# Delta-rule layers: tiles of 32 tokens of all four sequences in place of tiles of 128 tokens of one

## The reference

```
h = layer_norm(x, ln_g, ln_b)
qkvb = einsum('sbi,oi->sbo', h, slow_w).reshape(slen, bsz, H, 3 * D + 1)
q, k, v, beta = split(qkvb, [D, 2 * D, 3 * D])
q = softmax(q); k = softmax(k); beta = sigmoid(beta)
def step(W, inp):
    qt, kt, vt, bt = inp
    wk = einsum('bhde,bhe->bhd', W, kt)
    v_new = bt * (vt - wk)
    W = W + einsum('bhd,bhe->bhde', v_new, kt)
    return W, einsum('bhde,bhe->bhd', W, qt)
```

## Time and profile before

| | us |
|---|---|
| runs | 5360.01, 5378.66, 5394.14 |
| median | 5378.66 |
| span of the profiled execution | 5373.4 |
| TensorE busy | 4530.5 (84%), 57100 matmul records |
| VectorE busy | 2972.1 (55%) |
| ScalarE busy | 2152.0 (40%) |
| GpSimd busy | 831.7 (15%) |

### The profile page before, as it was taken

How to read it: one execution, slowest core, us unless ns; L and a number is a source line. 1 busy time by engine, 2 the same in 40 slices (tenths; PEclk the granted TensorE clock), 3 DMA queues, 4 the chain that set the end, 5 groups by cost and what they waited for, 6 DMA issues and landing times. The chain is left out here.

```text
span 5373.4 us, 139944 instructions
## 1 busy us (share of the span) xinstructions
PE 4530.5 (84%) x57100; PEld 2834.8 (53%) x57101; DVE 2972.1 (55%) x5849; ACT 2152.0 (40%) x4091; POOL 831.7 (15%) x2139
## 2 busy tenths in 40 slices
PE   3679898887997888897688886799999999984995
PEld 1237777773436777774355554354454545433663
DVE  3444444453024544454488886488686877852343
ACT  1133223232123333331466664277575766721221
POOL 0000000000000000000355553011111111104012
PEclk7788878798998988898899998899999999985997
DMA  1000000000000000000100000000000000006123
GB/s 42 2 7 3 3 3 3 3 3 18 0 0 9 4 3 3 3 4 3 38 1 1 1 1 0 10 1 1 1 0 1 0 1 1 0 3 217 61 84 101
DMA packets 47552, 85.70 MB, mean 16 GB/s; under 512 B 7121, under 2 KB 38129, under 8 KB 46065
## 3 DMA queue, kind: packets, MB, share of 16 engines
q1 hardware_dynamic: 40944, 61.84, 3.3%
q0 software_dynamic: 6144, 16.79, 1.0%
HBM read 45.05 MB, written 33.55 MB: 15 GB/s over the span
## 5 line engine op out<-in xcount | busy, mean ns | idle before, releaser
L1775 PE MATMUL psum<-hm_ex,hm_mix 128*128 128x512 f32 x1024 | 510.4, 621 | 42.3 <-ACT hm_Aq L1855 38.3
L1841 ACT ACTIVATE hm_ex<-psum,hm_nm 128x1024 f32<-128x1024 f32 x256 | 285.6, 1116 | 299.4 <-DVE hm_nm L1899 299.4
L1775 PEld LDWEIGHTS psum<-hm_ex,hm_mix 128*128 128x128 f32 x1024 | 175.6, 191 | 352.5 <-issue 344.8
L1914 DVE COPY hm_A<-psum 128x1024 f32<-128x1024 f32 x256 | 312.9, 1222 | 51.5 <-PE psum L1784 47.9
L1909 DVE TENSOR_SCALAR_CACHE_REDUCE hm_plus<-hm_Aq,hm_cbcol,hm_sums 128x1024 f32<-128x1024 f32 x256 | 340.5, 1330 | 0.0
L1899 DVE TENSOR_REDUCE hm_nm<-psum 128x1 f32<-128x1024 f32 x256 | 311.0, 1215 | 13.5 <-PE psum L1763 13.5
L1784 PEld LDWEIGHTS psum<-K,hm_Aq 128*128 128x128 f32 x2048 | 236.6, 140 | 150.0 <-issue 145.4
L957 DVE TENSOR_TENSOR fw_M<-fw_M,psum 128x256 f32<-128x256 f32 x256 | 107.8, 421 | 348.1 <-PE psum L728 345.6
L1846 ACT ACTIVATE hm_junk<-hm_Aq 128x1024 f32<-128x1024 f32 x256 | 270.6, 1057 | 30.3
L1763 PE MATMUL psum<-hm_kt,hm_qd 64*32 64x512 f32 x4096 | 280.1, 606 | 0.0
L1321 ACT ACTIVATE pt_signs<-pt_acts,pt_tb 128x1024 f32<-128x1024 f32 (+1 forms) x224 | 227.6, 1018 | 116.1 <-POOL pt_tb L1188 95.0
(11 more groups left out here) (379 smaller groups left out, 9044.6 us busy)
## 6 DMA issues: line engine op xcount, KB each, us to landing
ex_rows_in<-ex_zero SPq DMA_DIRECT2D x2, 5120.0 KB, 24.8
ex_xs<-ex_rows_in SPq DMA_DIRECT2D x80, 128.0 KB
ex_rows_out<-ex_ys SPq DMA_DIRECT2D x80, 128.0 KB, 1.7
ex_w<-in_ex_w SPq DMA_DIRECT2D x2, 4096.0 KB
X<-in_x SPq DMA_DIRECT2D x2, 2048.0 KB, 12.5
out_y<-X SPq DMA_DIRECT2D x2, 2048.0 KB, 9.0
ff_w<-in_ff_w SPq DMA_DIRECT2D x2, 1024.0 KB, 5.8
pt_w_proc<-in_pt_proc SPq DMA_DIRECT2D x1, 2048.0 KB, 7.6
```

What stands on the lines that cost most here:

```text
L1775: mm = pe.matmul(bank[4 + c], mix[:, u, :], ex[:, u, 512 * c:512 * c + 512], start=True, stop=True)
L1841: act.activation(ex[:, u, :], flat2(psum[:, 2 * u:2 * u + 2, :]), ACT.Exp, bias=nm[:, u:u + 1], accum_out=rsum[:, u:u + 1]).then_inc(s_ex, 1)
L1914: dve.tensor_copy(A[:, :, :, QT_ * t:QT_ * t + QT_], flat2(psum[:, 6:8, :]).rearrange("p (m g n) -> p m g n", m=MT, g=HEADS)).then_inc(s_a ...
```

## The change

A tile becomes 32 tokens of each of the four sequences: sequence b takes partitions 32b to 32b+31. The sequences are independent, so every product is a diagonal block of 32x32 for each head and sequence, and one step through the state serves a tile; there are still 32 tiles. The state M is compact, [128, 8, 32]; it starts at zero once, and `keep`, the zeroed operators and `spread` are gone. Keys and v are scaled by the square root of beta (GpSimd: (1 + e^-b) to the power -0.5), which makes the matrix symmetric; VectorE's 32x32 transpose takes the place of `turn`. The solve takes M's product with the keys into its right side (`u0`), so the keys are not solved. A body works on two tiles past the projection's (i and i-1) instead of three.

```diff
             for i in range(-1, 4):
-                body(i, i % 4, i + 1 < NT, i >= 0, i >= 1, i >= 2)
+                body(i, i % 4, i + 1 < NT, i >= 0, i >= 1)
...
-            for i in range(NT - 4, NT + 2):
+            for i in range(NT - 4, NT + 1):
...
+                        pool.tensor_copy(stage[:, :, :].rearrange("p h (b t) -> p h b t", b=B),
+                                         tokens(i + 1)).then_inc(s_staged, 1)
+                        pool.wait_ge(s_exp, i + 2)
+                        own.done(pool.tensor_tensor(eb[:, 1, :], eb[:, 0, :], power[:, 1, :], ALU.add))
+                        pool.tensor_tensor(eb[:, 2, :], eb[:, 1, :], power[:, 0, :], ALU.pow).then_inc(s_root, 1)
...
+                def tiles(to, by, of, sig, start=True, stop=True):
+                    for n in range(HEADS):
+                        for b in range(B):
+                            mm = pe.matmul(to(n)[rows(b), :], by(n)[rows(b), :], of(n)[rows(b), :],
+                                           start=start and (stop or n == 0), stop=stop)
...
-                def solve(by, of, sig):
-                    for n in range(HEADS):
-                        mm = pe.matmul(bank[2][:, 64 * n:64 * n + 64], by[:, n, :], of(n), start=True, stop=True)
-                    mm.then_inc(sig, 1)
...
+                product = lambda left, right: tiles(lambda n: bank[3][:, cols(n)], of(right), of(left), s_t)
+                chain = lambda by, moving, sig: tiles(lambda n: bank[4][:, cols(n)], by, of(moving), sig)
...
-                def spread(to, of, scale, sig):
-                    for c in range(4):
-                        last = act.activation(to[rows(c), :, rows(c)], of[rows(c), :, :], ACT.Copy, scale=scale)
-                    last.then_inc(sig, 1)
...
+                def softmax(i, a):
                     dve.wait_ge(s_exp, i + 1)
+                    own.done(dve.tensor_reduce(sm[:, :], groups(ex[:, :]), AX.X, ALU.add))
+                    own.done(dve.reciprocal(rs[:, :], sm[:, :]))
+                    dve.wait_ge(s_root, i + 1)
+                    own.mark(dve.tensor_tensor(split(vh[:, a, :]), split(bank[1][:, 0:C]), wide(eb[:, 2, :], HEADS),
                                                ALU.mult))
+                    own.done(dve.tensor_tensor(rs[:, HEADS:16], rs[:, HEADS:16], eb[:, 2, :], ALU.mult))
+                    own.done(dve.tensor_tensor(groups(qk[:, a, :]), groups(ex[:, :]), wide(rs[:, :], 16), ALU.mult))
+                    dve.transpose(qkT[:, a, :, :].rearrange("p n j -> p (n j)"), qk[:, a, :]).then_inc(s_qk, 1)
...
+                def solution(r, n, to, sig):
+                    dve.wait_ge(s_so, r * 4 + n)
+                    dve.tensor_tensor(flat(to[:, :, :]), bank[4][:, 0:C], flat(r0[:, :, :]), ALU.add).then_inc(sig, 1)
```

More of the change, by code:

```diff
@@ L606, in fast_weight_stage @@
[L606 to L615, removed]
+        eb = sb("eb", [P, 3, HEADS]); power = sb("power", [P, 2, HEADS])
@@ new lines, in fast_weight_stage @@
+        qk = sb("qk", [P, 4, QKN]); qkT = sb("qkT", [P, 4, 2 * HEADS, STEP])
+        vh = sb("vh", [P, 4, C])
+        compact = lambda n: sb(n, [P, HEADS, STEP])
+        l8, l8t, loff, z1, z2, tt, l2 = (compact(n) for n in "l8 l8t loff z1 z2 tt l2".split())
+        z3, nt, qm = (sb(n, [P, 2, HEADS, STEP]) for n in ("z3", "nt", "qm"))
+        u0, r0, rk, U, M, att = (compact(n) for n in "u0 r0 rk U M att".split())
+        names = ("w power staged pq pv dif exp root qk ga l8 lo qm t l2 z2 tt z3 nt th u0 so r0 rk u m up in att ot fin "
+                 "go dch pch").split()
@@ L644, in _, with body @@
             def _(pool):
-                off = k.const("off")[:, 0:DH].unsqueeze(1).broadcast_to([P, HEADS, DH])
-                def body(i, a, nxt, ch, so, rc):
+                own = Steps(pool, s_pch)
+                def body(i, a, nxt, ch, rc):
                     if nxt:
[L649 to L661, removed]
+                        if since(i, 0):
+                            pool.wait_ge(s_pv, i + 1)
+                        pool.tensor_copy(stage[:, :, :].rearrange("p h (b t) -> p h b t", b=B),
+                                         tokens(i + 1)).then_inc(s_staged, 1)
@@ L663, in _ @@
             @block.tensor
             def _(pe):
[L665 to L682, removed]
@@ L684, in gram @@
-                def gram(a, half, sig):
-                    for g in range(2):
-                        for c in range(4):
[L688 to L692, removed]
+                def tiles(to, by, of, sig, start=True, stop=True):
[3 more added lines that the diff above has]
+                                           start=start and (stop or n == 0), stop=stop)
+                    if sig is not None:
+                        mm.then_inc(sig, 1)
@@ L693, in gram, with project @@
+                def project(i, lo, hi, to, sig):
+                    for h in range(CH):
+                        mm = pe.matmul(bank[to][:, 0:hi - lo], stage[:, h, :], w[:, h, lo:hi],
+                                       start=(h == 0), stop=(h == CH - 1))
                     mm.then_inc(sig, 1)
-                def product(left, right):
+                def gram(a):
                     for n in range(HEADS):
-                        for b in range(4):
-                            mm = pe.matmul(bank[5][rows(b), DH * n:DH * n + DH], right[rows(b), n, :], left[rows(b), n, :],
+                        for b in range(B):
+                            mm = pe.matmul(bank[2][rows(b), 2 * STEP * n:2 * STEP * n + 2 * STEP],
+                                           qkT[rows(b), a, HEADS + n, :], qkT[rows(b), a, n:2 * HEADS:HEADS, :],
@@ L712, in through_state @@
[L712 to L741, removed]
-                    sa, ra = (a - 1) % 4, (a - 2) % 4
-                    given = lambda n: rhs[:, sa % 2, :, DH * (2 * (n % 4) + n // 4):DH * (2 * (n % 4) + n // 4) + DH]
-                    first = lambda n: r0[:, n, :, :]
-                    later = lambda n: rk[:, n, :, :]
-                    if rc:
-                        pe.wait_ge(s_ptc, r + 1)
-                        pe.wait_ge(s_m, r * 5 + 1)
-                        through_state(ra, 0)
-                    if so:
-                        pe.wait_ge(s_zx, s + 1)
-                        solve(z3x, given, s_y)
+                    mm.then_inc(s_ga, 1)
@@ L760, in body @@
+                        pe.wait_ge(s_u0, r + 1)
                         pe.sem_inc(s_go, 1)
-                        with_state(ra, 0)
-                    if ch:
-                        pe.wait_ge(s_ga, i + 1)
-                        pe.sem_inc(s_go, 1)
-                        gram(a, 1, s_gb)
-                    if so:
-                        pe.wait_ge(s_nt, s + 1)
-                        pe.wait_ge(s_r0, s + 1)
-                        solve(ntx, first, s_ap)
-                    if rc:
-                        pe.wait_ge(s_m, r * 5 + 2)
-                        through_state(ra, 1)
+                        chain(lambda n: z3[:, ru, n, :], u0, s_so)
@@ L799, in body @@
                     if rc:
-                        pe.wait_ge(s_u, r * 4 + 3)
+                        if since(r, 1):
+                            pe.wait_ge(s_att, r)
                         pe.sem_inc(s_go, 1)
-                        with_state(ra, 2)
-                    if so:
-                        pe.wait_ge(s_rk, s * 2 + 2)
-                        solve(ntx, later, s_ap)
+                        tiles(lambda n: bank[6][:, cols(n)], lambda n: qkT[:, ra, n, :], of(M), None, stop=False)
+                        pe.wait_ge(s_u, r + 1)
+                        pe.sem_inc(s_go, 1)
+                        tiles(lambda n: bank[5][:, cols(n)], lambda n: qk[:, ra, C + STEP * n:C + STEP * n + STEP],
+                              of(U), s_up)
                     if ch:
@@ L810, in body @@
                     if rc:
-                        pe.wait_ge(s_m, r * 5 + 4)
-                        through_state(ra, 3)
-                    if so:
-                        pe.wait_ge(s_pu, s + 1)
-                        turn_keys()
+                        for n in range(HEADS):
+                            for b in range(B):
+                                mm = pe.matmul(bank[6][rows(b), cols(n)], qm[rows(b), ru, n, :], U[rows(b), n, :],
+                                               start=False, stop=(n == HEADS - 1))
+                        mm.then_inc(s_in, 1)
                     if ch:
-                        pe.wait_ge(s_z, i * 2 + 2)
+                        pe.wait_ge(s_z3, i + 1)
                         pe.wait_ge(s_lo, i + 1)
                         pe.sem_inc(s_go, 1)
-                        product(z3, loff)
-                    if nxt:
-                        turn(i + 1, (a + 1) % 4)
+                        product(z3[:, a % 2], loff)
                     if rc:
-                        pe.wait_ge(s_u, r * 4 + 4)
-                        pe.sem_inc(s_go, 1)
```

(38 more changed lines are left out.)

237 lines of the change are left out of this document (86 added, 151 removed).

## The result

| kernel | median us | against the kernel before, in the same comparison |
|---|---|---|
| changed | 5467.6 (5463.7 to 5468.9) | 1.0167, interval 1.0133 to 1.0200 |
| before, in that comparison | 5372.6 | |

A forecast was written before the change was run, and what follows sets the result against it. TensorE's instruction packets bound the loop: 7.25 x 3.9 + 0.8 = 29.1 us a tile, 35 + 31.5 x 29.1 = 952 a layer, both 1903 against 1761.6, +142, hence 5520 us; range 5244 to 5793, rounded.

The forecast's parts named there:

- Packets of 250 records pace the loop: Delta-rule loops: TensorE takes its program in packets of 250 records and stops for nearly each; 7.25 packets a tile.
- T = 3.9: Delta-rule loops: T, the period of a packet that is waited for, taken as 3.9 us, giving 29.1 us a tile.
- The ends: Start and end of each delta-rule stage: 35 us before the steady tiles, then 31.5 tiles a layer.
- T's first part, "some 164 records of work": Within a packet's period: TensorE works some 164 records before the next packet is fetched, 0.96 to 1.4 us in dense groups.
- The second part: Within a packet's period: the wait from the packet showing until TensorE goes on, 2.4 to 2.9 us.
- Work lies under the packet: Delta-rule loops: engines alone need about 20 us a tile, 2.8 us a packet, hidden beneath the packet's period.
- The branch, 0.8 us a tile: Head of the 4-tile loop: its branch costs one further stop of 3.3 us for 4 tiles, 0.8 a tile.
- Rival 1: Delta-rule loops: packets cost under 2.8 us, the engines' 20 us a tile decide, -432 us, 4947 us; chance 0.10.
- Rival 2: Delta-rule loops: same packet mechanism at T of 3.3, dense groups shortening it; 24.7 us a tile, -134, 5244 us.
- Rival 3: Delta-rule loops: each packet takes 4.9 us, 36.3 us a tile, +597 us, 5975 us; chance 0.05.
- Rival 4: Delta-rule loops: the clock stays at 1.2 GHz, so halved work doesn't shorten the tile; 24 us a tile without packets (5200).
- Hidden costs: VectorE's transpose (0.69 us taken) and GpSimd's power (0.8 taken): claimed hidden under the time TensorE stands for packets.

The follow-up runs named there:

- e4: The changed kernel with its loop of 4 tiles an iteration written out, so TensorE doesn't branch within a stage: 5437.3 us, -30 against the changed kernel.
- e2: The changed kernel with the projection of queries and keys issued twice a tile (8 more records, about 2 us of TensorE's time): 5584.0 us, +116.
- e3: The changed kernel with the solve's operator nt spread into 128x128 blocks, three solve rounds of 8 wide matmuls instead of 32 small: 5605.0 us, +137.
- e7: The changed kernel with four extra 128x256 matmuls (8 records) a tile behind the product of z2, in a packet with slack: 5549.9 us, +82.
- e8: The kernel before the change with its loop written out: 5306.8 us against 5371.9 for the kernel before, ratio 0.9882.
- e12: The changed kernel, loop written out, with z2 times l2, the inside products and the state's update as wide matmuls: 5425.8 us, ratio to before 1.0089.

## Why the prediction was right

- *Packets of 250 records pace the loop.* Right: "issue", nearly all within L659, is the largest wait, 10 us a tile, and the waits for other engines are below 0.1 us a tile. The page *Runtime: NRT & Kernel Launch* of the Trainium skill, section "Instruction fetch mechanics", calls a crossing mostly hidden; here it is not (267 of 750 us). The same section of the Trainium skill says that a taken branch forces a fetch before the engine goes on, where its target lies outside the two blocks at hand; e4 agrees, with 30 us for 12 turns of a loop of some 29 packets.
- *T = 3.9.* A tile is 28.0 us, not 29.1; by the sum's own terms T is then (28.0 - 0.8) / 7.25 = 3.75 (the 3.8 of 750 / 197 also counts the stops at the branch). Over 31.5 tiles and two layers that is 69 us less than the 142 forecast. The ends cost 16 us more than estimated (a layer is 925 us, 35 + 31.5 x 28.0 is 917). 142 - 69 + 16 = 89, the measured difference of the stages. This term, T, is what was mis-sized; a step of 0.1 in it is 46 us. The rows it came from were too coarse: that no two packets stand closer than 4.0 was read from windows of 0.5 us, and the trace before has them start at 485.48, 489.15, 494.43 and 498.08, two of the three spacings 3.7.
- *T's first part, "some 164 records of work".* The mechanism I gave it was wrong. The packet is not fetched when so many records are done: over the loop it starts 1.0 to 1.8 us behind the point where TensorE goes on, in packets with a projection and in those without, and the step hardly follows the work between (0.08). So T is not work plus a wait but one length beside which the work goes on. The sum came out since 164 dense records happen to take 0.96 to 1.4 us; that was luck. The second part, 2.4 to 2.9 us, was right: 2.2 to 2.9.
- *Work lies under the packet.* Right for the small groups. A packet with a projection has little room left (0.54 us in the rows beside e2), and e2 and e3 fell over that.
- *The branch, 0.8 us a tile.* The sum charged it to all 63 tiles, 50 us; the loops hold 48, which would be 38, and e4 measured 30.
- *Rival 1, packets keep up:* ruled out by the waits. The first half of its premise may hold, as the next packet starts soon after TensorE enters the present one; but it takes 3.8 us in all and not under 2.8. *Rival 2,* T of 3.3: T lies between it and the forecast, and the reason given, that dense groups shorten it, is what the slope of 0.08 speaks against. *Rival 3,* 4.9 us a packet: too long. *Rival 4:* the clock does stay low, 0.65, but the packets set the tile; e7 shows what the clock does to work that is paid, 3.78 us instead of 1.99.
- *Hidden costs.* The transpose took 0.71 us (0.69 taken), the power 1.64 (0.8 taken); VectorE's waits name neither, as forecast:

```profile
L821 DVE STREAM_TRANSPOSE fw_qkT<-fw_qk 128x512 f32<-128x512 f32 x26 | 18.5, 711 | 0.9
```

```profile
L647 POOL TENSOR_TENSOR fw_eb<-fw_eb,fw_power 128x8 f32<-128x8 f32 x26 | 42.5, 1636 | 2.0
```

## What to carry to other kernels

Count TensorE's records as well as its busy time: where "issue" stops it at equal counts, a change that cuts the work but adds instructions can lose (here a fifth less busy time, 45% more records). In this kernel a packet of 250 records cost the longer of its own work and 3.8 us, so wide matmuls with few records pay where small ones stand in a row, and cost their full time beside long ones. A loop's branch cost 2.5 us a turn here; where a program may grow, writing the loop out is cheap to try.

## What the runs showed of the hardware that was not expected

A packet that TensorE waits for comes about every 3.8 us however little the last one held (steps of 3.4 to 4.2 us over work of 1.4 to 3.5), while the instruction queue is busy 1.8% of 16 engines' time; what sets the 1.0 to 1.8 us before the next one starts, and the 2.2 to 2.9 from there, stays open. In the changed stages TensorE stood 35% of the time at a granted clock of 0.65, and in e7 the same eight records took 1.99 or 3.78 us. That the stops lower the clock isn't shown: in e8 and e12 TensorE stood 10% of the same 700 us, and the granted clock was 0.93 in the one and 0.67 in the other.
